# First batch's product of rows formed tile by tile, projection norms in halves of the rows, and waits inside chains in the plan

## The reference, cut to what matters

```python
xn  = (x - mean) / sqrt(var + eps)                    # layer norm, per row
att = (xn Wtheta^T)(xn Wphi^T)^T / 16                 # no softmax: linear
x1  = x + att (xn Wg^T)                               # = x + xn Wtheta^T Wphi (xn^T xn) Wg^T / 16

xh  = layernorm(x1);  h = rmsnorm(xh) * ln1
q, k, v = split(h Wqkv^T)                             # 16 heads, 4 key/value heads, 16 wide; rotary on q and k
x2  = xh + softmax_causal(q k^T / 4) v Wo^T
h2  = rmsnorm(x2) * ln2
top2 of softmax(h2 Wgate^T) over 8 experts, weights renormalised
out = x1 + x2 + sum over the two experts of weight * (silu(h2 W1^T) * (h2 W3^T)) W2^T
```

## Time and profile before

| | us |
|---|---|
| median of 3 runs | 1151.1 |
| the profiled execution | 1150.42 |
| its span | 1148.7 |
| TensorE busy | 1086.8 (95%) |
| VectorE busy | 730.9 (64%) |
| ScalarE busy | 576.9 (50%) |
| GpSimd busy | 406.9 (35%) |
| mean granted TensorE clock | 0.987 |

### The profile page before, as it was taken

How to read it: one execution, slowest core, us unless ns; L and a number is a source line. 1 busy time by engine, 2 the same in 40 slices (tenths; PEclk the granted TensorE clock), 3 DMA queues, 4 the chain that set the end, 5 groups by cost and what they waited for, 6 DMA issues and landing times.

```text
span 1148.7 us, 20388 instructions
## 1 busy us (share of the span) xinstructions
PE 1086.8 (95%) x7126; PEld 680.8 (59%) x7126; DVE 730.9 (64%) x1414; ACT 576.9 (50%) x1108; POOL 406.9 (35%) x476
## 2 busy tenths in 40 slices
PE   6989999999999899998999998999999999999997
PEld 5766444553445333353344443446666999999996
DVE  4596968568675977667876679524464555555553
ACT  4544576547566687665466665564321323223230
POOL 1020233344552244221444511545527733333332
PEclk9999999999998999999999999999999999999999
DMA  5334023223234366550343231224334422222220
GB/s 172 111 123 123 13 63 95 70 70 100 74 115 137 133 185 214 144 160 24 89 124 89 86 112 33 55 57 89 88 74 99 100 48 47 49 48 43 45 42 11
DMA packets 85716, 102.06 MB, mean 89 GB/s; under 512 B 17104, under 2 KB 73296, under 8 KB 85616
## 3 DMA queue, kind: packets, MB, share of 16 engines
q1 hardware_dynamic: 71312, 81.13, 24.2%
q0 software_dynamic: 14304, 19.63, 9.1%
HBM read 55.89 MB, written 41.01 MB: 84 GB/s over the span
## 4 chain that ended last, share of the span: by engine, by line
PE 72%; DVE 18%; issue 3%; ACT 3%; DMA 2%; POOL 1%; SPq 1%; DVEq 0%; POOLq 0%; ACTq 0%
PE psum L1932 14%; PE psum L1948 10%; PE psum L1877 9%; PE psum L1863 7%; DVE mx L1676 7%; PE psum L1924 7%; PE psum L1850 4%; PE psum L1845 4%; PE psum L1884 2%; PE psum L1831 2%; PE psum L1785 2%; PE psum L1807 2%; ACT probs_mem L1224 2%; PE psum L1851 1%; PE psum L1912 1%
## 5 line engine op out<-in xcount | busy, mean ns | idle before, releaser
L1676 DVE TENSOR_REDUCE mx<-psum 128x1 f32<-128x640 f32 (+6 forms) x352 | 345.3, 1022 | 90.9 <-PE psum L1851 85.9
L1224 ACT ACTIVATE probs_mem<-psum 128x512 f32<-128x512 f32 (+1 forms) x608 | 308.3, 584 | 164.5 <-PE psum L1863 162.8
L1085 POOL TENSOR_SCALAR_AFFINE_SELECT probs_mem<-probs_mem 128x512 f32<-128x512 f32 x128 | 81.7, 639 | 342.3 <-ACT probs_mem L1224 342.2
L1130 POOL DMA_INDIRECT out<-yout,labels x71 | 112.1, 1578 | 221.2 <-DVE yout L1742 169.5
L1863 PE MATMUL psum<-stack_mem 98*128 98x512 bf16 (+3 forms) x768 | 174.7, 328 | 11.0 <-DVE mx L1676 5.0
L1877 PE MATMUL psum<-probs_mem,v 128*17 128x512 f32 (+3 forms) x1536 | 160.9, 496 | 1.1 <-ACT probs_mem L1224 0.5
L1850 PE MATMUL psum<-stack_mem 96*128 96x256 bf16 (+3 forms) x448 | 127.9, 317 | 5.7 <-DVE mx L1676 3.3
L1863 PEld LDWEIGHTS psum<-stack_mem 98*128 98x128 bf16 x768 | 64.3, 98 | 93.5 <-DVE mx L1676 33.1
L1845 PE MATMUL psum<-stack_mem 96*128 96x512 bf16 x256 | 98.8, 391 | 10.6 <-DVE mx L1676 7.6
L1924 PE MATMUL psum<-w_mem,blockT 128*128 x200 | 95.6, 600 | 4.5 <-DVE blockT L1726 2.1
L1851 PE MATMUL psum<-causal,identb 128*128 128x128 bf16 x448 | 97.3, 223 | 0.0
(11 more groups left out here) (207 smaller groups left out, 1498.7 us busy)
## 6 DMA issues: line engine op xcount, KB each, us to landing
block<-routed SPq DMA_DIRECT2D x71, 129.0 KB, 2.1
w_mem<-in_w13T SPq DMA_DIRECT2D x16, 512.0 KB, 4.3
qk_parts<-w_mem SPq DMA_DIRECT2D x16, 384.0 KB, 2.7
stack_mem<-qk_parts SPq DMA_DIRECT2D x32, 192.0 KB, 3.1
w_mem<-in_x SPq DMA_DIRECT2D x8, 512.0 KB, 4.9
out<-w_mem SPq DMA_DIRECT2D x8, 512.0 KB, 4.0
x_late<-out SPq DMA_DIRECT2D x8, 512.0 KB, 5.1
stack_mem<-qk_parts SPq DMA_DIRECT2D x32, 128.0 KB, 2.7
```

The lines of the kernel that those rows point to most:

```text
L1085: e.affine_select(pb[:, :, q0:q0 + P], pb[:, :, q0:q0 + P], [[0, GRP], [1, P]], ALU.is_ge, 0.0, base=0, channel_multiplier=-1).then_inc(se ...
L1130: e.indirect_dma_start(out_rows, bass.IndirectOffsetOnAxis(ap=labels[w % NLABEL].bitcast(I32)[:, 0:1], axis=0), youts[w % NYOUT], None, bo ...
L1224: e.activation(probs[m % 2][:, hh:hh + n, q0:CH], grid(turn[step][0][:, 0:n * (CH - q0)], n), ACT.Exp, scale=float(HD) ** -0.5).then_inc(s ...
L1676: e.tensor_reduce(to, took, AX.X, ALU.max).then_inc(sem["max"], 1)
```

## The change

`norm1` and `norm2` are done for tiles 0 to 3 and then for tiles 4 to 7, each half a full chain, so that there are 26 and 28 instructions a batch in place of 13 and 14; `aggr` and `aggr2` wait for their own tile's statistics only, `xn` and `h` for their half's norm. For batch 0, `gram` has 8 units of one tile each (both halves of the result, in two banks of PSUM) in place of two units over all tiles; the other batches keep theirs. `needs` now names the step before in each chain (and the step before at the half's border in others), `route`'s planned duration goes from 0.13 to 0.11. `project` is eleven streams in place of one, with `square` and `gram` ahead of `xnT`, and `v` last. The first head's first maxima get an earlier due time and the second half's a later one. `load_x` of batch 0 is planned to land in 4.0 us in place of 7.0, `SPACING` goes from 4.0 to 3.5. Idle matmuls after `prepare` are two bfloat16 matmuls over 64 rows each into two banks, where a pair of banks is free. In the diff the returns of `route` in `needs` are left out: each gains `+ earlier`; `norm1` and `norm2` keep their instructions, on half the columns.

```diff
+HALF = TPB // 2
+def gram_steps(b):
+    return KD if b else TPB
...
-LATENCY, COLD = 0.05, 0.1
+LATENCY, COLD, FIRST_ROWS = 0.05, 0.1, 4.0
...
-    "route": (("DVE", 0.13),)
+    "route": (("DVE", 0.11),)
...
     if stage == "gram":
-        return (("PE", 3.46), ("ACT", 0.49)) if at[1] else (("PE", 3.46),)
+        took = ("PE", 0.865 * TPB / gram_steps(at[0]))
+        return (took, ("ACT", 0.49)) if at[1] == gram_steps(at[0]) - 1 else (took,)
...
-SPACING = 4.0
+SPACING = 3.5
...
         if stage == "pair":
-            return [("weights",)]
+            return [("load_x", 0)]
...
         if stage == "norm1":
-            return [("aggr", b, TPB - 1)]
+            return [("aggr", b, HALF * (at[1] // NORM1_STEPS + 1) - 1)] + [(stage, b, at[1] - 1)] * (at[1] > 0)
...
         if stage == "gram":
-            return [("xn", b, TPB - 1)] + [("x1", b - 1, TPB // 2 - 1)] * (b > 0)
+            return [("xn", b, TPB - 1 if b else at[1])] + [("x1", b - 1, TPB // 2 - 1)] * (b > 0 and not at[1])
...
         if stage == "norm2":
-            return [("aggr2", b, TPB - 1)]
+            return [("aggr2", b, HALF * (at[1] // NORM2_STEPS + 1) - 1)] + [(stage, b, at[1] - 1)] * (at[1] > 0)
         if stage == "h":
-            return [("norm2", b, NORM2_STEPS - 1)]
+            return [("norm2", b, NORM2_STEPS * (at[1] // HALF + 1) - 1)] + in_order(step)
         if stage == "hT":
-            return [("h", b, 2 * at[1] + 1)]
+            return [("h", b, 2 * at[1] + 1), ("x1", b, TPB // 2 - 1)] + in_order(step)
...
         if stage == "norm3":
-            return [("square_sum", b, TPB - 1)] + [("h2", b - 1, TPB - 1)] * (b > 0)
+            return [("norm3", b, at[1] - 1)] * (at[1] > 0) + [("square_sum", b, TPB - 1)] + [("h2", b - 1, TPB - 1)] * (b > 0)
...
         if stage == "route":
+            earlier = [("route", b, at[1] - 1)] * (at[1] > 0)
             ... each return with + earlier
...
     def project(b):
+        steps = [(0, ("load_x", b))]
+        for half in range(2):
+            tiles = range(half * HALF, (half + 1) * HALF)
+            steps += [(half, (s, b, j)) for s in ("stats", "aggr") for j in tiles]
+            steps += [(half, ("norm1", b, half * NORM1_STEPS + i)) for i in range(NORM1_STEPS)] + [(half, ("xn", b, j)) for j in tiles]
+        steps += [(2, ("gram", b, i)) for i in range(gram_steps(b))] + [(2, ("square", b, i)) for i in range(2)]
+        steps += [(3, ("xnT", b, c)) for c in range(TPB // 2)] + [(4, ("prepare",))] * (b == 0)
         for i in range(TPB // 2):
+            steps += [(3, ("x1", b, i)), (5, ("stats2", b, 2 * i)), (5, ("stats2", b, 2 * i + 1))]
+        for half in range(2):
+            tiles = range(half * HALF, (half + 1) * HALF)
+            steps += [(6 + half, ("aggr2", b, j)) for j in tiles] + [(6 + half, ("norm2", b, half * NORM2_STEPS + i)) for i in range(NORM2_STEPS)]
+            steps += [(6 + half, ("h", b, j)) for j in tiles] + [(8 + half, ("hT", b, half * HALF // 2 + c)) for c in range(HALF // 2)]
+            steps += [(8 + half, (s, b, half)) for s in ("k_mm", "q1_mm", "q2_mm")]
+        return steps + [(10, ("v", b))]
...
     def maxima():
...
-            yield from spread_over((n - 1) * KTS, (n - 1) * KTS + 10, steps)
+            first = len(max_units(0)) + 1 if n == 0 else 0
+            yield from spread_over(-KTS, -KTS + 2, steps[:first])
+            yield from spread_over((n - 1) * KTS + KTS * (n == 0), (n - 1) * KTS + 10, steps[first:])
...
             def norm1(b):
+                for half in range(2):
+                    s, m = (v[:, b % 2][:, :, half * HALF:(half + 1) * HALF] for v in (rt, mv.rearrange("p s t c -> p s c t")))
+                    q.wait_ge("aggr", TPB * b + HALF * (half + 1))
...
                 if stage == "warm":
-                    q.wait_ge("load_eye", 16)
-                    e.matmul(bk[:, 0:P], ident, ident, start=True, stop=True)
+                    if place[step][1] == 2:
+                        q.wait_ge("const", 4)
+                        for i in range(2):
+                            rows_of = slice(i * P // 2, (i + 1) * P // 2)
+                            e.matmul(grid(bk[:, i * CH:i * CH + 2 * P], 2), identb[rows_of], causal[rows_of].unsqueeze(1).broadcast_to([P // 2, 2, P]), start=True, stop=True)
...
                 elif stage == "gram":
-                    b, k = at
-                    bk = turn["gram", b, 0][0]
-                    q.wait_ge("xn", TPB * (b + 1))
-                    for j in range(TPB):
-                        m = e.matmul(bk[:, k * D:(k + 1) * D], xn[b % 2][:, j, k * P:(k + 1) * P], xn[b % 2][:, j], start=(j == 0), stop=(j == TPB - 1))
+                    b, i = at
+                    to = gram_parts(b)
+                    q.wait_ge("xn", TPB * (b + 1) if b else i + 1)
+                    for j, k in [(j, i) for j in range(TPB)] if b else [(i, k) for k in range(KD)]:
+                        m = e.matmul(to[:, k], xn[b % 2][:, j, k * P:(k + 1) * P], xn[b % 2][:, j], start=(j == 0), stop=(j == TPB - 1))
                     m.then_inc(sem["gram_mm"], 1)
```

More of the change, by code:

```diff
@@ L221, in gated_free, with in_order @@
         return [("down", w - NGATED)] if w - NGATED >= STAGED else [("gatedT", STAGED - 2)]
+    def in_order(step):
+        stage, b, i = step
+        first = HALF // 2 if stage == "hT" else HALF
+        return [(stage, b, i - 1)] if i == first else []
     def needs(step):
@@ L479, in plan @@
         first, last = PROJECT_DUE[b]
-        streams.append((spread_over(first, last, project(b)), False))
+        steps_of = list(spread_over(first, last, project(b)))
+        for n in range(11):
+            streams.append((iter([(due, step) for due, (of, step) in steps_of if of == n]), False))
         streams.append((iter([(last, ("x1_store", b))]), False))
@@ L487, in plan @@
         streams.append((spread_over(at, at + 8, [("base", b, j) for j in range(TPB)]), False))
-    per_batch = {"load_x": 1, "x1_store": 1, "x1_load": 1, "stats": TPB, "aggr": TPB, "norm1": NORM1_STEPS, "xn": TPB, "xnT": TPB // 2, "gram": KD, "square": 2, "x1": TPB // 2,
-                 "stats2": TPB, "aggr2": TPB, "norm2": NORM2_STEPS, "h": TPB, "hT": TPB // 2, "v": 1, "k_mm": QR, "q1_mm": QR, "q2_mm": QR,
+    per_batch = {"load_x": 1, "x1_store": 1, "x1_load": 1, "stats": TPB, "aggr": TPB, "norm1": 2 * NORM1_STEPS, "xn": TPB, "xnT": TPB // 2, "gram": 0, "square": 2, "x1": TPB // 2,
+                 "stats2": TPB, "aggr2": TPB, "norm2": 2 * NORM2_STEPS, "h": TPB, "hT": TPB // 2, "v": 1, "k_mm": QR, "q1_mm": QR, "q2_mm": QR,
                  "split": 15 * QR, "split_store": 3 * QR, "xhat": TPB, "wo": TPB, "base": TPB, "square_sum": TPB, "norm3": NORM3_STEPS, "h2": TPB,
@@ L495, in seat @@
     def seat(step):
-        n = max_banks(*step[3:]) if step[0] == "max" else 1
+        n = max_banks(*step[3:]) if step[0] == "max" else KD if step[:2] == ("gram", 0) else 1
         at = min(range(RING - n + 1), key=lambda i: max(empty[i:i + n]))
@@ L525, in keep_warm @@
             steps.append(step)
-            place[step] = free[0], 1
+            pairs = [i for i in free if i % 2 == 0 and i + 1 in free] if done.get(("prepare",), NEVER) < at else []
+            place[step] = (pairs[0], 2) if pairs else (free[0], 1)
             clock["PE"] = at + WARM_TOOK
@@ L553, in plan @@
             if known[n] is None:
-                if len(step) > 1 and count.get(step[0], 0) < per_batch.get(step[0], 0) * step[1]:
+                if step[0] == "gram" and count.get("gram", 0) < sum(gram_steps(b) for b in range(step[1])) or (
+                        len(step) > 1 and count.get(step[0], 0) < per_batch.get(step[0], 0) * step[1]):
                     continue
@@ L616, in plan @@
         else:
-            done[step] = end + DRAIN[engine] + LANDING.get(step[0], 0.0)
+            done[step] = end + DRAIN[engine] + (FIRST_ROWS if step == ("load_x", 0) else LANDING.get(step[0], 0.0))
         if in_ring and engine in ("DVE", "ACT") and all(e not in ("DVE", "ACT") for e, _ in chain[i + 1:]):
@@ L1152, in _ @@
                     o = b % 2
[L1153 to L1154 removed]
+                    q.wait_ge("norm2", NORM2_STEPS * (2 * b + j // HALF + 1))
+                    q.wait_ge("gram_mm", nth["gram", b, gram_steps(b) - 1])
                     q.wait_ge("xnT_mm", TPB // 2 * (b + 1))
```

95 lines of the change are left out of this document (43 added, 52 removed).

## The result

The changed kernel took 1117.41 us (median of 4 runs, 1115.85 to 1118.43) against 1150.37 us, ratio 0.9692, 95% interval 0.9631 to 0.9753; once more, beside other experiments, 0.9704 (0.9671 to 0.9737). It is faster by 33 us.

The account below looks back on a forecast made before the run. TensorE, busy 95% of the span, was taken as the bound, with time to gain only where it waits or runs at half clock. 1150.4 - 9 (start) - 12 (chains) + 3 (added work) = 1132.4, forecast 1133 us, range 1118 to 1155.

Parts of the forecast that it names:

- Chains in the attention: Attention: ready maxima go between dependent steps, cutting TensorE's idle and half-clock time; 12 us saved, bounds 0 and 25.
- Start, first half: Batch 0 up to gram: gram tile by tile ends at about 17.3, not 23.5 us; 6 us saved.
- Second half: Batch 0 from x1 to k: norm2 in halves brings k earlier, up to 5.3 us; 3 us taken.
- The start's worth: Batch 0's start, both halves together: 9 us saved, bounds 0 and 13.6; first score at or before 91.
- Added work: Extra norm1 and norm2 steps on VectorE from halving: 3 us lost, bounds 0 and 8.2.
- Behind the attention: After the attention ends: 11.9 us of TensorE idle time seen there, no gain in the sum.
- Only the start: Rival: the chains' stalls in the attention stay and only the start gains; 1145 us, chance 0.23.
- The rule of the Trainium skill: VectorE chains: each instruction waits for the pipe to empty anyway, so leaving out semaphores saves nothing; chains' part zero.
- Given back: Rival: VectorE's added steps from 50 to 84 us give the start's gain back; 1153 us, chance 0.12.
- Steps held by GpSimd: Rival: norm steps of batches 1 to 3 held beside GpSimd's splits; 1166 us, decides above 45 steps, chance 0.09.

Follow-up runs that it names:

- experiment 1: Kernel before, with only the plan's knowledge of the step before added in norm1, norm2, norm3 and route: 0.9943, 1147.18 us.
- experiment 9: Kernel before, with the chain's wait known to the plan in norm3 and route only: 0.9895, 1140.79 us.
- experiment 11: Changed kernel with idle matmuls allowed only from 10 us of the plan's time (5 before): 0.9689, 1115.18 us; repeated, 0.9674, 1115.09 us.
- experiment 4: Changed kernel with batch 0's gram back in two units over all tiles, after the last xn: 0.9789, 1131.97 us.
- experiment 3: Changed kernel with the scatters' SPACING back at 4.0 from 3.5 us: 0.9729, 1121.77 us.
- experiment 2: Changed kernel with the waits of all chains unknown to the plan and route's step back at 0.13 us: 0.9975, 1150.52 us.
- 8: Changed kernel with waits unknown in norm1 and norm2 only: 0.978, 1128.71 us; in norm3 and route only, route at 0.13 us: 0.9911, 1146.68 us.
- experiment 6: Kernel before, with chains' waits known and project() split into streams, no halves, gram whole, SPACING 4.0: 0.9841, 1137.63 us.

## Why the prediction was wrong

**The way was right, the sum too small**: 18 us forecast, 33 measured. By place, in lost TensorE time: the start gave 1.7 us in place of 9, the attention 25.9 in place of 9 (chains 12, added work -3), and 4.0 came from behind it, where nothing was forecast. The first error hides a part of the second.

**Chains in the attention, forecast 12, bounds 0 and 25.** This is the step that failed, by its size, together with the term beside it that took 3 us off for added steps. The direction holds: taken out, the plan's knowledge costs 33 us, most of it at norm3 and route. The 12 came from "about half of VectorE's delay goes", a share of VectorE's time used for TensorE's. TensorE doesn't wait for the chain to be over but for a maximum behind it, as at 378.58 us before. In the changed kernel route's steps are spread over 43 us (351 to 394) where they took 26 before (373 to 399), and TensorE is idle less, not more. Lost time from 105 to 800 us fell by 25.9 us, slightly over the upper bound: idle time from 34.8 to 14.3 us, the clock's loss, in windows of 5 us, from 8.5 to 1.7.

Knowledge alone does not do this. In the kernel before it took 8.6 us off the same stretch (experiment 1; 17.1 with norm3 and route alone, experiment 9), with 28.4 us still idle. So for the part by itself 12 was not far off. What the sum lacked is that the parts need each other: it added them as if each were worth the same alone and together.

**Start, first half, forecast 6.** Failed. "It ends at about 17.3" was 21.8. The xn came near the time forecast, but the plan's own idle matmuls stood in TensorE's order. Without them it ended at 19.5 and 20.9 (experiment 11), later than 17.3 too, because its first records took 1.7 times as long; the prediction had 0.87 us a tile from the start. Neither could be seen in the trace before, only that the plan fills gaps with idle matmuls. **Second half, forecast 3**: k was 5.0 us earlier beyond x1's 2.2, so it was undersized, near the upper end of its bracket (5.3). The first score was at 90.84, as forecast (91 or before).

**The start's worth, 9.** Up to 105 us the lost time fell by only 1.7 us; earlier milestones were bought with work moved behind them, which the prediction had named but not applied to its own term. Yet gram by tiles is worth 0.9789 against 0.9692 (some 11 us), more than the 6 us. Not because gram itself is earlier: it ended 1.8 us before the old time. With chains known, the first batch loses more (7.4 us more up to 105 us in experiment 1), and with gram whole the order puts idle matmuls and a copy ahead of its last xn (experiment 4). Gram by tiles got rid of that order; this was luck as far as the prediction goes, since no term had it.

**Added work, forecast minus 3.** Wrong in sign as a net: halves are worth some 17 us in the changed kernel (0.9848 against 0.9692 and 0.9704). VectorE was busy 6.4 us longer than before, 4.4 us longer than with norms whole, where 10 to 20 were named as a sign.

**Behind the attention, forecast nothing.** 4.0 us less lost behind 800 us, and one more block in the attention. Not in the sum. The spacing of the scatters, put at nothing, may hold 3 to 4 us (experiment 3), which isn't settled.

**Rivals.** Only the start: refuted by experiment 2. The rule of the Trainium skill (VectorE: DVE Perf Modes, section "The DRAIN you can't avoid") by which this part would be zero went with it: in the earlier trace rows an unrelated instruction starts 0.08 us after a step, and experiments 1, 2 and 8 show that what the plan sets between two steps decides. Given back: in the terms of TensorE's lost time it is near the truth for the start (1.7 us of 9 left up to 105 us), but not by its VectorE price, for VectorE was busy 31.80 of the 34 us from 50 to 84, against 31.66, and the first score came 9.1 us earlier. Steps held by GpSimd: 11 of 264 norm steps took over 0.3 us, 6.4 us over 0.17 together, where 45 were needed; one of the longest, with the instruction beside it:
```profile
245.98 1.27 POOL L1102 TENSOR_TENSOR w_mem<-w_mem 64x512 f32<-64x512 f32 x1 [9.63 <-DVE w_mem L1674]
246.13 1.15 DVE L1354 TENSOR_SCALAR rt<-mv 128x4 f32<-128x4 f32 x1
```
With norms whole it was 17 of 156 and 11.3 us, and in the kernel before 10 of 156 and 5.0 us: more steps did not mean more of them held.

**What stays open.** Why a faster attention alone leaves TensorE with idle matmuls behind it. They follow the number of experts' blocks already used up in the attention: with nine none (before), with ten 0 to 3.0 us (none in the changed kernel and experiment 3, 3.0 in experiment 6), with eleven 8.2 (experiment 1), with twelve 11.2 (experiment 9). Fewer blocks are then left for the time until the last batch's rows are routed; this was not tested apart. The spacing is not the reason, since with 4.0 us there are none there either. How halves lower the attention's loss by 17 us was measured, not traced to a wait. The first maxima's due times, the planned landing of the first rows and the new idle matmuls were never taken out by themselves; with the chains unknown they and all the rest gave nothing (experiment 2).

## What to carry to other kernels

In a fixed order, a dependent chain of small instructions has to be planned with its waits, or it is stacked ahead of the work that another engine waits for. Account for the bound engine as work plus idle plus lost clock plus filler: it shows at once whether a part removed a loss or only turned it into the planner's own gaps. Filler in a fixed order is not free: it can stand ahead of real work, or ahead of what another engine needs first (experiment 4). Such parts don't add: measure each by taking it out of the whole as well as by putting it in alone.

## What the runs showed of the hardware

With independent instructions between a chain's steps, most of a step's wait costs VectorE no busy time. The same 108 more steps cost it 17.4 us, 0.16 us each, where the plan stacked them (experiment 2, busy 748.3 against 730.9 us), and 6.4 us, 0.06 each, where it set others between (the changed kernel, 737.3 us); with the waits known, another order of the same steps was busy 741.5 (experiment 4). A row of the chain alone shows 0.20 us from step to step.

A matmul record of 128x256 f32 took 634 ns on the mean from 12.5 to 14.5 us where gram followed 1.2 us of idle time, and 379 ns from 15 to 17 us where it followed idle matmuls (experiment 11).
